# A Mamba block with experts on one core: the last row product of a block added to the sums by an accumulating DMA

## The chip, the cores and the metric

The kernel runs on one core of a Trainium2 chip, in one launch. The core's engines run side by side, each through its own list of instructions in order: TensorE (PE: matmuls and transposes; its weight loads are shown as PEld), VectorE (DVE), ScalarE (ACT), GpSimd (POOL) and SyncE (SP), which here only starts DMAs. They meet through semaphores alone: an instruction that waits holds up all that stands behind it on its engine. The metric is the time of one execution on the device in microseconds (us), lower is better.

## The reference

Only what bears on the change is kept. `x` has 16 sequences of 256 tokens by 256 features, E is 512, N is 16.

```python
xn = layernorm(x)
hidden, gate = split(einsum('blh,he->bel', xn, W_in), 2)
hidden = silu(causal_conv4(hidden) + conv_bias)              # 512 channels x 256 tokens
dt, B, C = split(hidden^T @ W_x, [128, 144])                 # 128, 16 and 16 columns
dts = softplus(dt @ W_dt + b_dt)
...
state[n] = exp(dts * A[n]) * state[n] + dts * B[n] * hidden  # a scan over tokens, for each n of 16
scan_out = sum over n of state[n] * C[n]
y = (scan_out + hidden * D) * silu(gate)
out = x + y^T @ W_out + experts(xn)                          # 32 experts, top 8, gate, up and down
```

All is float32. `experts` is computed densely: the 32 experts' 96 columns stand side by side as 24 tiles of 128, taken as 12 pairs.

## The kernel before

A block is one sequence. There are 16 of them, and their work is laid out in 128 slots a block (8 for each of the 16 states n). Every engine walks the same slots, and tables of numbers (`ROW_ADD_AT`, `WEIGH_AT` and others) say at which slot of which block each step stands in that engine's list. A table has three rows: for the first block, the fourteen in the middle, and the last. Slots under 0 belong to the block's early work and run while the block ahead is in its slots 0 to 127; slots of 128 and over run in the block behind. So slot -16 of the next block is slot 112 of this one, and slot 136 of this block is slot 8 of the next. The slots give an order and no time.

A state n goes like this. ScalarE makes the decays (`decays`, L657). GpSimd makes the input `du * B[n]` into one of four buffers (`state_input`, L571, `state[:, n % STATES]`, STATES is 4, 128 partitions x 1024 numbers). VectorE scans it in two halves (`scan`, L878). Then C[n] is applied in one of two ways. Eight states, 0 among them, go by turning: TensorE transposes them (`turn`, L1100) and VectorE multiplies and adds them into `acc` (`add_state`, L884). The other eight are the row states 2, 4, 5, 6, 8, 9, 10 and 12. For states 5 and 9 VectorE multiplies (L912) and adds (L919) from `decay`, which lies in PSUM. For states 2, 4, 6, 8, 10 and 12 GpSimd multiplies the state by a row of C laid over all partitions (`state_output`, L580), and VectorE adds the product, 128x1024, into the sums `u2` of the block (`add_row`, L891). Both inputs of that addition lie in SBUF. The sums are formed in a fixed order, `ROW_SUMS`, in which 12 is the last, behind 10. `y_sum` (L927) adds what was turned, GpSimd multiplies by the gate (`gated`, L591), and TensorE projects (`project_y`, L1148).

The buffer of state 12 is buffer 0. The next one to fill it is state 0 of the next block, at slot 112, and `state_input` waits there until the product of 12 has been added. `step_input` (L554, `du = u * dt` of the next block) stands just ahead of it on GpSimd, at slot 111. `weigh` (L586) multiplies a pair of expert tiles by their router weights, on GpSimd too. `norm` (L539 to L545) is GpSimd's part of the next block's normalization and waits for VectorE's `moments` (L826). `load_c` (L643) starts the loads of the rows of C from ScalarE's queue, and waits until GpSimd has made the product that used the buffer before.

Of the kernel before, what the change touches and what calls it, by code (L numbers as in the profile page):

```python
# [33 lines left out]
def build(nc, x_d, w_in_d, conv_k_d, conv_b_d, w_x_d, w_dt_d, b_dt_d, w_out_d, a_log_d, d_d,  # L34
# [33 lines left out]
    STATES = 4  # L68
# [45 lines left out]
    ROW_ADD_AT = [[42, 54, [45, 47], 70, 80, [76, 79], 106, 116], [37, 49, [44, 47], 61, 78, [76, 76], 102, 119], [30, 51, [43, 44], 64, 78, [75, 76], 102, 153]]  # L114
# [16 lines left out]
    ROWS_BY_VECTOR = [n for n in BY_ROW if n in ((5, 9))]  # L131
    ROW_SUMS = sorted(BY_ROW, key=lambda n: n if n in ROWS_BY_VECTOR else n + ROW_LAG)
# [19 lines left out]
    with ExitStack() as ctx:  # L152
# [6 lines left out]
        def sem(name):  # L159
            return ctx.enter_context(nc.semaphore(name))  # L160
# [133 lines left out]
        row_added = sem("row_added")  # L294
        row_summed = sem("row_summed")
# [75 lines left out]
        def row_at(i, n):  # L371

            of = [k for k in BY_ROW if k not in ROWS_BY_VECTOR]
            return i * len(of) + of.index(n) + 1

# [26 lines left out]
        def wait_summed(eng, i, k, h=1):  # L402

            if k < 0:
                eng.wait_ge(skip_ready, i + 1)
            elif ROW_SUMS[k] in ROWS_BY_VECTOR:
                eng.wait_ge(row_summed, row_half(i, ROW_SUMS[k], h))
            else:
                eng.wait_ge(row_added, row_at(i, ROW_SUMS[k]))

# [115 lines left out]
        def _(pool):  # L526
# [29 lines left out]
            def state_input(i, q, n):  # L556
# [6 lines left out]
                if not (isinstance(i, int) and i == 0 and n < STATES):  # L563
                    before, at = (n - STATES) % NS, (i if n >= STATES else i - 1)
                    if before in ROWS_BY_VECTOR:
                        pool.wait_ge(scanned, half_at(at, before, 1))
                    elif before in BY_ROW:
                        pool.wait_ge(row_added, row_at(at, before))
                    else:
                        pool.wait_ge(turned, turn_at(at, before, 1))  # L570
# [3 lines left out]
            def state_output(i, n):  # L574
# [5 lines left out]
                pool.tensor_tensor(x, x, c_rep[:, r % ROWS, :][:, None, :].broadcast_to([P, ET, T]), ALU.mult).then_inc(row_ready[0], 1)  # L580

# [11 lines left out]
            def slot(i, q, a):  # L593
# [8 lines left out]
                if a == POOL_ALONE[s]["rstd"]:  # L602
                    norm(i)
                if a == POOL_ALONE[s]["select"]:
                    select(i)
# [205 lines left out]
        def _(dve):  # L811
# [128 lines left out]
            def slot(i, q, a):  # L940
# [22 lines left out]
                for n, at in zip(BY_ROW, ROW_ADD_AT[s]):  # L963
                    if n not in ROWS_BY_VECTOR and a == at:
                        add_row(i, q, n)
# [250 lines left out]
```

## Time and profile before

| | us |
|---|---|
| median of 3 runs | 1341.82 |
| lowest and highest | 1341.73, 1341.94 |
| the profiled execution | 1342.44 |
| its span (first to last instruction) | 1340.6 |
| one block in the middle, by `gated` at 701.11 and 781.49 | 80.38 |
| TensorE busy in such a block (703.1 to 783.5) | 79.76 |
| VectorE, GpSimd, ScalarE busy in it | 76.66, 75.67, 75.15 |

The profiled execution took 1.8 us more than its span. The first block ramps up for some 60 us, the last ends at the end of the span, and the blocks between repeat each other. Busy times of TensorE come from modelled ends of pipelined matmuls. The clock granted to TensorE was full (0.999 as the mean of the span).

In a row of a timeline, "x2" means that two like instructions are merged; a bracket gives the engine's idle time just before and the instruction that ended it. ACTq and SPq are the queues of ScalarE and SyncE, whose DMA starts are rows of their own. A line's number is that of the kernel before.

### The profile page before, as it was taken

The page shows a single profiled execution, that of the slowest core. Times are in us where ns is not written, and L with a number is a line of the kernel's source. Part 1 is how long each engine was busy: PE and PEld are TensorE (multiplying, and loading weights), DVE is VectorE, ACT ScalarE, POOL GpSimd, SP SyncE. Part 2 cuts the span into 40 slices and gives each one's busy share as a digit, 9 for nine tenths or more (in the row PEclk, how much of TensorE's full clock was granted, in tenths as well). Part 3 has the DMA queues.
Part 4 walks back from the last instruction along what each step waited for, and adds up shares of the span by engine and source line. Part 5 has one row for each costly group of instructions (what it writes and reads, how often), then busy time and mean ns, then how long its engine had stood idle before and what let it go on. Part 6 is the DMA issues. An engine that isn't in the chain of part 4 may idle for free.

```text
span 1340.6 us, 26644 instructions
## 1 busy us (share of the span) xinstructions
PE 1301.6 (97%) x9222; PEld 1219.6 (91%) x9222; DVE 1239.6 (92%) x1644; ACT 1213.2 (90%) x2111; POOL 1233.9 (92%) x674
## 2 busy tenths in 40 slices
PE   6899999999999999999999999999999999999998
PEld 5889999999999999999999999999999899999987
DVE  3799999999999999999999999999999999999997
ACT  5879999999999999999999999999999899999984
POOL 2999999999999989999999999989999999999996
PEclk9999999999999999999999999999999999999999
DMA  7543443544444344443544444344443534434342
GB/s 193 160 144 118 143 120 115 152 115 132 139 127 135 112 136 127 139 120 118 149 120 126 136 128 138 114 132 131 139 122 116 148 114 134 139 113 142 109 146 80
DMA packets 189399, 174.95 MB, mean 130 GB/s; under 512 B 43185, under 2 KB 172241, under 8 KB 189265
## 3 DMA queue, kind: packets, MB, share of 16 engines
q1 hardware_dynamic: 150864, 121.86, 30.5%
q10 hardware_dynamic: 38400, 51.40, 13.6%
q8 instruction: 73, 1.20, 0.4%
q14 instruction: 62, 0.50, 0.1%
HBM read 167.92 MB, written 5.24 MB: 129 GB/s over the span
## 4 chain that ended last, share of the span: by engine, by line
POOL 27%; issue 21%; ACT 19%; DVE 18%; PE 12%; DMA 2%; ACTq 1%; SPq 0%; DVEq 0%; POOLq 0%
POOL state L571 14%; POOL moe L586 6%; ACT decay L657 5%; PE pair_ps L1003 5%; ACT L657 5%; ACT L665 4%; DVE state L878 4%; PE out_ps L1138 3%; POOL state L580 3%; DVE dt L865 3%; DVE u L891 2%; DVE decay L878 2%; DVE u L919 2%; ACT moe L665 2%; DVE moe L898 2%
## 5 line engine op out<-in xcount | busy, mean ns | idle before, releaser
L571 POOL TENSOR_TENSOR state<-du,b_rep 128x1024 f32<-128x1024 f32 x256 | 611.7, 2395 | 61.1 <-DVE u L891 59.3
L878 DVE TENSOR_TENSOR_SCAN state<-decay,state 128x512 f32<-128x512 f32 x448 | 534.2, 1212 | 21.1 <-ACT decay L657 16.4
L657 ACT ACTIVATE decay<-dt,neg_a 128x255 f32<-128x255 f32 x1024 | 436.7, 465 | 37.7 <-DVE state L878 19.0
L1138 PE MATMUL out_ps<-w_down,moe 128*128 128x256 f32 x1536 | 355.9, 381 | 3.1 <-POOL moe L586 1.9
L1138 PEld LDWEIGHTS out_ps<-w_down,moe 128*128 128x128 f32 x1536 | 282.5, 190 | 38.6 <-issue 4.1
L586 POOL TENSOR_TENSOR moe<-moe,rw_rep 128x512 f32<-128x512 f32 x192 | 249.3, 1309 | 8.7 <-DVE moe L898 7.3
L580 POOL TENSOR_TENSOR state<-state,c_rep 128x1024 f32<-128x1024 f32 x96 | 244.1, 2543 | 1.6 <-DVE state L878 1.6
L1003 PE MATMUL pair_ps<-xnT_hi,w_gate_hi 128*128 128x256 f32 x768 | 228.9, 298 | 3.2 <-DVE moe L898 3.2
L1003 PE MATMUL pair_ps<-xnT_hi,w_up_hi 128*128 128x256 f32 x768 | 225.7, 294 | 2.8 <-ACT moe L665 1.9
L657 ACT ACT_TABLE_LOAD x171 | 219.4, 1283 | 2.5
L1003 PE MATMUL pair_ps<-xnT_lo,w_gate_hi 128*128 128x256 f32 x768 | 216.4, 282 | 0.0
L1003 PE MATMUL pair_ps<-xnT_hi,w_gate_lo 128*128 128x256 f32 x768 | 216.0, 281 | 0.0
L1003 PE MATMUL pair_ps<-xnT_hi,w_up_lo 128*128 128x256 f32 x768 | 215.8, 281 | 0.0
L1003 PE MATMUL pair_ps<-xnT_lo,w_up_hi 128*128 128x256 f32 x768 | 215.7, 281 | 0.0
L665 ACT ACT_TABLE_LOAD x144 | 184.8, 1283 | 5.3 <-PE out_ps L1138 1.7
L884 DVE SCALAR_TENSOR_TENSOR acc<-turn_ps,c_tok,acc 128x512 f32<-128x512 f32 x224 | 160.4, 733 | 3.3 <-PE turn_ps L1100 2.1
L1003 PEld LDWEIGHTS pair_ps<-xnT_hi,w_up_hi 128*128 128x128 f32 x768 | 144.6, 188 | 12.2 <-ACT moe L665 8.1
L1003 PEld LDWEIGHTS pair_ps<-xnT_hi,w_gate_hi 128*128 128x128 f32 x768 | 145.3, 189 | 7.3 <-DVE moe L898 5.7
L891 DVE TENSOR_TENSOR u<-u,state 128x1024 f32<-128x1024 f32 x96 | 149.0, 1552 | 0.8 <-POOL state L580 0.2
L898 DVE TENSOR_TENSOR moe<-moe,pair_ps 128x512 f32<-128x512 f32 x192 | 129.2, 673 | 20.9 <-PE pair_ps L1003 20.9
L1003 PEld LDWEIGHTS pair_ps<-xnT_lo,w_gate_hi 128*128 128x128 f32 x768 | 145.4, 189 | 0.8
L1003 PEld LDWEIGHTS pair_ps<-xnT_hi,w_gate_lo 128*128 128x128 f32 x768 | 145.4, 189 | 0.0
(149 smaller groups left out, 2252.5 us busy)
## 6 DMA issues: line engine op xcount, KB each, us to landing
w_down<-in_L_ffn_w_down_dram SPq DMA_DIRECT2D x384, 128.0 KB, 2.9
b_rep<-b_dram ACTq DMA_DIRECT2D x128, 256.0 KB, 3.3
rw_rep<-rw_dram SPq DMA_DIRECT2D x256, 96.0 KB, 2.7
c_rep<-b_dram ACTq DMA_DIRECT2D x128, 128.0 KB, 3.3
rw_rep<-rw_dram SPq DMA_DIRECT2D x256, 64.0 KB, 2.6
rw_rep<-rw_dram SPq DMA_DIRECT2D x256, 32.0 KB, 2.6
x_in<-L_attn_input_states_dram SPq DMA_DIRECT2D x16, 256.0 KB, 3.8
res<-L_attn_input_states_dram SPq DMA_DIRECT2D x16, 256.0 KB, 3.1
```

The costliest lines, as they stand in the source:

```text
L571: pool.tensor_tensor(state[:, n % STATES, :, :], du2[:, q, :, :], b_rep[:, n // BCH % 2, n % BCH, :][:, None, :].broadcast_to([P, ET, T]), ...
L580: pool.tensor_tensor(x, x, c_rep[:, r % ROWS, :][:, None, :].broadcast_to([P, ET, T]), ALU.mult).then_inc(row_ready[0], 1)
L586: pool.tensor_tensor(moe[:, p % RING, :, :], moe[:, p % RING, :, :], rw_rep[:, p % WEIGHTS, :, :], ALU.mult).then_inc(pair_weighed[0], 1)
L657: last = act.activation(decay[:, h, j, 1:T], dt[:, q, e, 1:T], ACT.Exp, scale=neg_a[:, e, n:n + 1])
L665: act.activation(moe[:, p % RING, :, :], bank(p, 0), ACT.Silu).then_inc(pair_silu, 1)
L865: last = dve.scalar_tensor_tensor(out=x, in0=ps[:, j, 0:T - shift], scalar=conv_k[:, e, k:k + 1], in1=x, op0=ALU.mult, op1=ALU.add)
L878: dve.tensor_tensor_scan(a if n in ROWS_BY_VECTOR else x, a, x, 0.0, ALU.mult, ALU.add).then_inc(scanned, 1)
L884: dve.scalar_tensor_tensor(out=acc[:, c, :], in0=turn_ps[:, c, :], scalar=c_tok[:, q, c, NS + n:NS + n + 1], in1=acc[:, c, :], op0=ALU.mul ...
L891: dve.tensor_tensor(u2[:, q, :, :], u2[:, q, :, :], state[:, n % STATES, :, :], ALU.add).then_inc(row_added, 1)
L898: dve.tensor_tensor(m, m, bank(p, 1), ALU.mult).then_inc(pair_mul, 1)
L1003: last = pe.matmul(out, w(a, k), x(b, k), start=(at == 0), stop=(at == len(terms) - 1))
L1138: last = pe.matmul(out_ps[:, c, :], moe[:, p % RING, j, c * P:(c + 1) * P], w_down[:, p % RING, j, :], start=(p == 0 and j == 0 and c == 0 ...
```

## The change

The product of state 12 is no longer added by VectorE. GpSimd starts a DMA that reads `state[:, 0]` and adds it into `u2` in SBUF (`accum_op`), 128 partitions of 4 KB. It does so for each of the 16 blocks. A new semaphore, `row_moved`, tells when it has landed. What waited for the addition of 12 waits for it now: `state_input` of state 0 of the next block, and `y_sum`. The DMA start itself waits for the sum of row 10 (VectorE) and for GpSimd's own product of 12. It stands at slot 106, 102 or 118 (first, middle, last blocks), where VectorE's addition stood at 116, 119 or 153.

```diff
-    ROW_ADD_AT = [[42, 54, [45, 47], 70, 80, [76, 79], 106, 116], [37, 49, [44, 47], 61, 78, [76, 76], 102, 119], [30, 51, [43, 44], 64, 78, [75, 76], 102, 153]]
+    ROW_ADD_AT = [[42, 54, [45, 47], 70, 80, [76, 79], 106, 106], [37, 49, [44, 47], 61, 78, [76, 76], 102, 102], [30, 51, [43, 44], 64, 78, [75, 76], 102, 118]]
...
+    ROWS_BY_DMA = [n for n in BY_ROW if n in ((12,))]
...
+        def moved_at(i, n):
+
+            return (i * len(ROWS_BY_DMA) + ROWS_BY_DMA.index(n) + 1) * 16
...
+            elif ROW_SUMS[k] in ROWS_BY_DMA:
+                eng.wait_ge(row_moved, moved_at(i, ROW_SUMS[k]))
...
+                    elif before in ROWS_BY_DMA:
+                        pool.wait_ge(row_moved, moved_at(at, before))
...
+            def move_row(i, q, n):
+
+                wait_summed(pool, i, ROW_SUMS.index(n) - 1)
+                row_multiplied(pool, i, n)
+                pool.dma_start(u2[:, q, :, :], state[:, n % STATES, :, :], accum_op=ALU.add).then_inc(row_moved, 16)
...
+                for n, at in zip(BY_ROW, ROW_ADD_AT[s]):
+                    if n in ROWS_BY_DMA and a == at:
+                        move_row(i, q, n)
...
                 for n, at in zip(BY_ROW, ROW_ADD_AT[s]):
-                    if n not in ROWS_BY_VECTOR and a == at:
+                    if n not in ROWS_BY_VECTOR and n not in ROWS_BY_DMA and a == at:
                         add_row(i, q, n)
```

GpSimd's list in a middle block, from the product of 12 (the first row) to state 0 of the next block (the last), before. L571 makes state inputs, L586 weighs.

```order
L580 TENSOR_TENSOR state<-state,c_rep 128x1024 [waits c_loaded1,scanned]
L571 TENSOR_TENSOR state<-du,b_rep 128x1024 [waits row_added,b_loaded1]
L586 TENSOR_TENSOR moe<-moe,rw_rep 128x512 [waits pair_mul,rw_loaded0]
L586 TENSOR_TENSOR moe<-moe,rw_rep 128x512 [waits pair_mul,rw_loaded1]
L571 TENSOR_TENSOR state<-du,b_rep 128x1024 [waits turned]
L554 TENSOR_TENSOR du<-u,dt 128x1024 [waits dt_ready]
L571 TENSOR_TENSOR state<-du,b_rep 128x1024 [waits row_added,b_loaded0,du_ready]
```

The same place after:

```order
L590 TENSOR_TENSOR state<-state,c_rep 128x1024 [waits c_loaded1,scanned]
L581 TENSOR_TENSOR state<-du,b_rep 128x1024 [waits row_added,b_loaded1]
L602 TENSOR_TENSOR moe<-moe,rw_rep 128x512 [waits pair_mul,rw_loaded0]
L596 DMA u<-state 128x1024 [waits row_ready_by_pool,row_added]
L602 TENSOR_TENSOR moe<-moe,rw_rep 128x512 [waits pair_mul,rw_loaded1]
L581 TENSOR_TENSOR state<-du,b_rep 128x1024 [waits turned]
L562 TENSOR_TENSOR du<-u,dt 128x1024 [waits dt_ready]
L581 TENSOR_TENSOR state<-du,b_rep 128x1024 [waits row_moved,b_loaded0,du_ready]
```

The DMA start came in between two weighings, with one weighing, one state input and `du` between it and the instruction that waits for it. In the first block it stands one place on, behind the state input of 15, with only a weighing and `du` behind it. The second place is the end of VectorE's list in the last block, before (L891 is the addition of row 12, L927 is `y_sum`):

```order
L891 TENSOR_TENSOR u<-u,state 128x1024 [waits row_ready_by_pool,row_added]
L884 SCALAR_TENSOR_TENSOR acc<-turn_ps,c_tok,acc 128x512 [waits added,turned]
L898 TENSOR_TENSOR moe<-moe,pair_ps 128x512 [waits pair_silu,up_in]
L884 SCALAR_TENSOR_TENSOR acc<-turn_ps,c_tok,acc 128x512 [waits added,turned]
L898 TENSOR_TENSOR moe<-moe,pair_ps 128x512 [waits pair_silu,up_in]
L927 TENSOR_TENSOR u<-u,turn_ps 128x512 [waits row_added,y_turned] x2
```

and after:

```order
L917 TENSOR_TENSOR moe<-moe,pair_ps 128x512 [waits pair_silu,up_in]
L903 SCALAR_TENSOR_TENSOR acc<-turn_ps,c_tok,acc 128x512 [waits added,turned]
L917 TENSOR_TENSOR moe<-moe,pair_ps 128x512 [waits pair_silu,up_in]
L946 TENSOR_TENSOR u<-u,turn_ps 128x512 [waits row_moved,y_turned] x2
```

The addition is gone from the list, and `y_sum` waits for `row_moved` in place of `row_added`. The lists of TensorE, ScalarE and SyncE are the same in both kernels.

## Rows read from the trace of the kernel before

**Rows 1.** Busy times by stretch, one middle block; columns in the first line.

```profile
core 0: us, PE busy (x) PEld busy (x) DVE busy (x) ACT busy (x) POOL busy (x), PEclk, DMA share, GB/s
703.10:783.50 80.40, 79.76 (x569) 74.87 (x568) 76.66 (x104) 75.15 (x132) 75.67 (x42) 1.00 0.43 128
```

**Rows 2.** The chain that ended last, 700 to 800 us: start, us, what.

```profile
743.60 1.24 DVE u L891
...
744.96 0.51 POOL state L571
...
775.40 0.21 POOL var_eps L539
...
787.47 2.34 POOL state L580
789.88 0.33 ACTq L643
```

**Rows 3.** Timeline of GpSimd in one middle block: start, us, instruction.

```profile
754.43 3.38 POOL L580 TENSOR_TENSOR state<-state,c_rep 128x1024 f32<-128x1024 f32 x1
...
760.11 2.52 POOL L586 TENSOR_TENSOR moe<-moe,rw_rep 128x512 f32<-128x512 f32 x2
762.59 2.38 POOL L571 TENSOR_TENSOR state<-du,b_rep 128x1024 f32<-128x1024 f32 x1
764.93 3.34 POOL L554 TENSOR_TENSOR du<-u,dt 128x1024 f32<-128x1024 f32 x1
768.35 7.11 POOL L571 TENSOR_TENSOR state<-du,b_rep 128x1024 f32<-128x1024 f32 x3
```

**Rows 4.** Timeline of VectorE in the same block.

```profile
754.12 1.44 DVE L891 TENSOR_TENSOR u<-u,state 128x1024 f32<-128x1024 f32 x1
...
763.86 2.19 DVE L891 TENSOR_TENSOR u<-u,state 128x1024 f32<-128x1024 f32 x1
765.98 1.21 DVE L878 TENSOR_TENSOR_SCAN state<-decay,state 128x512 f32<-128x512 f32 x1
...
774.74 0.25 DVE L826 BATCH_NORM_AGGREGATE moments<-stats 128x2 f32<-128x6 f32 x2
...
776.01 1.26 DVE L927 TENSOR_TENSOR u<-u,turn_ps 128x512 f32<-128x512 f32 x2
```

**Rows 5.** Durations min/median/max in ns over the whole run, three lines.

```profile
L554 POOL TENSOR_TENSOR du<-u,dt x16: 2357/3342/3382, 37.3 to 1247.8; 128x1024 f32<-128x1024 f32 x16
L891 DVE TENSOR_TENSOR u<-u,state x96: 1197/1394/2276, 69.9 to 1325.9; 128x1024 f32<-128x1024 f32 x96
L445 SPq DMA_DIRECT2D x_in<-L_attn_input_states_dram x16: 428/432/979, 0.7 to 1111.8; - x16
```

**Rows 6.** DMA issues: count, KB each, median us from issue to landing.

```profile
u<-in_L_attn_W_in_dram SPq DMA_DIRECT2D x1, 512.0 KB, 4.3
gate<-in_L_ffn_w_up_dram SPq DMA_DIRECT2D x1, 384.0 KB, 6.9
neg_a<-in_L_attn_A_log_dram SPq DMA_DIRECT2D x1, 32.0 KB, 2.3
```

**Rows 7.** Busy times of a 4 us stretch, columns as in rows 1.

```profile
761.00:765.00 4.00, 4.00 (x36) 3.98 (x35) 4.00 (x5) 3.96 (x5) 4.00 (x4) 1.00 0.40 118
```

**Rows 8.** GpSimd's timeline at the end of the first block.

```profile
119.72 1.30 POOL L586 TENSOR_TENSOR moe<-moe,rw_rep 128x512 f32<-128x512 f32 x1
```

**Rows 9.** GpSimd's timeline at the end of the last block.

```profile
1322.87 2.40 POOL L580 TENSOR_TENSOR state<-state,c_rep 128x1024 f32<-128x1024 f32 x1
1328.54 2.54 POOL L586 TENSOR_TENSOR moe<-moe,rw_rep 128x512 f32<-128x512 f32 x2 [3.28 <-DVE moe L898]
1331.17 2.35 POOL L591 TENSOR_TENSOR u<-u,gate 128x1024 f32<-128x1024 f32 x1
```

**Rows 10.** VectorE's timeline there.

```profile
1329.81 1.28 DVE L927 TENSOR_TENSOR u<-u,turn_ps 128x512 f32<-128x512 f32 x2 [0.15 <-PE turn_ps L1110]
```

**Rows 11.** The chain that ended last, there: start, us, what.

```profile
1333.66 3.65 PE out_ps L1148 x16
```

More of the change, by code:

```diff
@@ L294, in build @@
         row_added = sem("row_added")
+        row_moved = sem("row_moved")
         row_summed = sem("row_summed")
@@ L371, in row_at @@
         def row_at(i, n):
-            of = [k for k in BY_ROW if k not in ROWS_BY_VECTOR]
+            of = [k for k in BY_ROW if k not in ROWS_BY_VECTOR and k not in ROWS_BY_DMA]
             return i * len(of) + of.index(n) + 1
+        def moved_at(i, n):
+            return (i * len(ROWS_BY_DMA) + ROWS_BY_DMA.index(n) + 1) * 16
         def read_a(i, name):
```

## The prediction

> **What bounds the kernel now.** Read the middle blocks first, since fourteen of the sixteen are alike. In one of them TensorE is busy for 79.76 of 80.40 us, and VectorE, ScalarE and GpSimd for some 75 to 77 [rows 1]. So nothing can win more than 0.6 us a block, TensorE's whole idle time, and there is no engine with much to spare for a loss either. The busy shares don't say which engine sets the pace, and the chain of waits does. In each block it comes from VectorE's addition of a row at 743.60 to GpSimd at 744.96, stays on GpSimd (apart from pieces named "issue", which lie inside instructions of GpSimd) until its product of row 2 ends at 789.8, and goes on to ScalarE's queue, whose start of a load of C waits for that product [rows 2]. In those 45 us GpSimd's timeline has no idle bracket; the stretch that the change touches, 754 to 775, is in the middle of it [rows 3]. A microsecond more of GpSimd there is a microsecond more for the block, and a microsecond less is worth at most 0.4: VectorE delivers the moments at 774.99, GpSimd picks them up at 775.40 [rows 2, 4], and from there on GpSimd would wait.
>
> **What the addition costs now.** VectorE's 128x1024 addition takes 1.2 us by itself (minimum 1197 ns) [rows 5]. At 763.86 it took 2.19, and GpSimd's `du`, begun at 764.93, took 3.34 in place of 2.36 [rows 3 to 5]. The times fit a turn-taking: the addition begins while GpSimd still runs the state input of 762.59 to 764.97, does its work only after that (764.97 to 766.05), and `du` starts in earnest only then. The same pair is at 754.12 and 754.43 (3.38 in place of 2.36). The median of `du` is 3342 ns over 16 blocks, so nearly every block pays this 1.0 us, on the path. The Trainium skill (SBUF — State Buffer, section "Who interferes with whom") states this: a VectorE instruction with two SBUF inputs and a GpSimd instruction that reads SBUF exclude each other. By that rule, the trace agrees, and the scans, whose decays lie in PSUM, cost GpSimd nothing.
>
> **What the change takes away.** On VectorE 2.19 us a block. It is not on the path: behind it stands the scan of state 15 (765.98), whose input GpSimd finishes at 764.97 now. On GpSimd 1.0 us a block, the waiting of `du`. It is on the path.
>
> **What it adds on GpSimd: the DMA's start (call it g).** The trace of before has no DMA begun by GpSimd. Nearest below: starts on the hardware queues of the other two, 0.33 us on ScalarE's [rows 2] and 0.43 on SyncE's [rows 5]. Nearest above: a whole GpSimd instruction over the same tile, 2.37 [rows 3]. Less than 0.33 is not likely, since GpSimd's work over a tile takes twice VectorE's time (2.36 to 1.20) [rows 5]. I scale SyncE's 0.43 by that 2, and by 1.5 because an accumulating transfer names three operand streams (two read, one written) against two: 1.3, and I take 1.2. Its two waits are met: row 10 was added by 755.56, and the product of 12 ended at 757.81, while the start would fall at 761.4, between the two weighings of 760.11. What is queued behind it is the second weighing, the input of 15, `du`, and state 0 of the next block. All of it moves by g - 1.0 = 0.2 us by the time state 0 starts. The input of 15 itself moves from 764.97 to 766.2, which holds VectorE's scan to 766.2 where it began at 765.98: VectorE gets nothing of its 2.19 us here.
>
> **What it adds as a wait: the landing (L, from the beginning of the start).** A load of 512 KB landed 4.3 us after issue and one of 32 KB took 2.3 [rows 6]. That leaves 2.0 for the data. The accumulating one reads both operands, so I double that: 2.3 + 4.0 = 6.3, plus 0.8 by which GpSimd's start is longer than SyncE's: L = 7.1. Bounds: 4.3 if reading twice costs nothing and the start is short; 2.3 + 2 x 4.6 = 11.5 if the worst large load of the trace (6.9, rows 6) is what it meets [rows 6]. Ahead of state 0 there is g, a weighing 1.25, an input 2.35 and `du` 2.36 (freed of its waiting), that is g + 6.0 = 7.2 us. So in a middle block the DMA lands 0.1 us before it is needed. That is no margin: past it, each us of L is a us of wait on GpSimd, on the path. The other waiter, `y_sum` at 776.01 [rows 4], has over 7 us of room. The removed addition had 2.3 us of room there (ended 766.05, needed 768.35).
>
> A page gives another price. The Trainium skill (DMA: Bandwidth & Descriptors, section "Anatomy of one DMA — SWDGE (gpsimd) path") puts a DMA begun by GpSimd at about 2.0 us plus its bytes at 436 GB/s, an estimate of 3.2 us here, and its specifications give about 1 us to the first byte. No run here shows it; it is weighed as a rival below, there worked out from rows.
>
> **The two ends.** First block: only a weighing 1.25 and `du` 2.36 stand between the start and state 0 [rows 5, 8], so the room is g + 3.6 = 4.8, the wait 2.3, and with the 0.2 of above 2.5 us. Last block: the product of 12 ends at 1325.27 and GpSimd has nothing to do until 1328.54, so g is free there, but the sum is needed by `y_sum`, which began at 1329.81, and `gated` and the projection follow at once (1331.17 + 2.35 = 1333.52, projection at 1333.66) [rows 9 to 11]. The DMA lands at 1325.27 + 7.1 = 1332.4, so `y_sum` is 2.6 late, of which 0.14 is room: 2.4 us. VectorE's addition did this in 1.22 us. Here is the one place where the latency of the DMA is in full on the path.
>
> **The sum.** Fourteen middle blocks x 0.2 = 2.8; first block 2.5; last block 2.4; together 7.7. On the profiled execution's 1342.44 that is 1350.1. The median of the runs is 0.6 below the profiled one, so 1349.5, that is 0.6% slower. The two blocks at the ends carry more than half of it.
>
> **The rivals.** (1) The start is as short as on the hardware queues. With g = 0.4 GpSimd gets 0.6 us a block, of which 0.4 counts before VectorE's moments hold it. The point from which the sign turns is g = 0.6 or so, as 14 x (g - 1.0) must pay for the ends. With L = 4.8 the first block pays 0.2 and the last 0.1. Sum 14 x -0.4 + 0.3 = -5.3, so 1336.5. For it: TensorE's 0.6 idle us allow it, and VectorE's freed 2.19 us could help where I see no use for them. Against: everything must go right, and GpSimd's programs are slow elsewhere in the trace. (2) Break-even: g = 1.0 and a landing within the room in all blocks. The ends then cost nothing when L is under 4.5 (1325.27 + 4.5 = 1329.8), the middle nothing: 1341.8. For it: the transfer begins where the DMA engines are 0.40 busy [rows 7], and 512 KB landed in 4.3 at the start of the run, where loads crowd. Against: an accumulate reads twice as much. The Trainium skill (the page and section above) leads to this case, with its estimate of 3.2 us. (3) The transfer is late: state 0 waits in every block. With L 1.5 us longer than mine, 8.6, the room of 7.2 is passed by 1.4, so 14 x 1.4 + 2 x 1.5 = 22.6 more: 1372. For it: it begins with no margin, a large load has taken 6.9 [rows 6], and the kernel's own loads take 0.44 of the DMA engines' time [rows 1] and share them. (4) The start itself is as long as a full instruction, g = 2.4: 14 x 1.4 = 19.6, and 5 at the ends: 1366, with the room grown to 8.4 so that no landing is waited for.
>
> **Chances.** My forecast and its neighbourhood (1345 to 1358) 0.38; (3) and (4) together 0.22, both slower; (2) 0.20, within 0.2%; (1) 0.20, faster. I take 0.2% (2.7 us) as what a measurement of this kernel can tell from no change. The range goes from 1336, the floor of (1), to 1371: over it lie the landings that are later still, up to 11.5, some 1 in 10, and under it less than 1 in 10. Faster 0.20, same 0.20, slower 0.60.
>
> **What the profile of the changed kernel would show.** The first thing to read is the row of GpSimd's DMA start, its duration g, and how far the next weighing begins after the last one ended. `du` at 2.36 in place of 3.34 in the middle blocks shows the freed microsecond; if it stays at 3.3, another addition has moved onto it. An idle bracket of GpSimd before state 0, released by the DMA, would show a late landing, and its absence would kill (3). The step between two `gated` instructions, 80.38 now, should be 80.6; under 80.1 is (1). In the last block the idle bracket before `y_sum` should name the DMA, with about 2.5 us. The forecast is wrong if GpSimd's stretch from 745 to 790 gets idle time of another cause, for then it did not set the pace.

## The result and the profile after

| | before | after |
|---|---|---|
| median of the runs, us | 1341.83 | 1355.15 |
| lowest and highest | 1341.73, 1341.94 | 1354.07, 1355.86 |
| the profiled execution, and its span | 1342.44, 1340.6 | 1354.85, 1353.0 |
| step from `gated` to `gated`, the block shown | 80.38 | 81.04 (709.07 to 790.11) |
| median of the 12 steps from the second to the thirteenth | 80.40 | 81.04 |
| first `gated` | 137.79 | 139.77 |
| last step | 68.13 | 69.11 |

The changed kernel is slower: ratio 1.0099, 95% interval 1.0081 to 1.0116. The direction and the range were right; the forecast of 1349.5 was 5.7 us short. Executions of one kernel differ by up to some 5 us with the mean clock granted to TensorE: on the chip of experiments 9 to 12 the kernel before has a median of 1342.57 us in its 19 executions at 0.999 or more and of 1347.72 in its 7 at 0.996 or less. Line numbers below are those of the changed kernel unless said otherwise: `state_input` is L581, `state_output` L590, the DMA start L596, `weigh` L602, `du` L562, the load of B L654, the decays L676, SiLU L684, the experts' matmul L1022.

The page of after, busy time and the issues of the new DMA (count, KB each, median us from issue to landing):

```profile
PE 1302.9 (96%) x9222; PEld 1219.0 (90%) x9222; DVE 1210.8 (89%) x1628; ACT 1213.2 (90%) x2111; POOL 1234.2 (91%) x690
...
u<-state POOLq DMA_DIRECT2D x16, 512.0 KB, 5.7
```

GpSimd's timeline in a middle block, the place of [rows 3]:

```profile
762.38 3.40 POOL L590 TENSOR_TENSOR state<-state,c_rep 128x1024 f32<-128x1024 f32 x1
765.72 2.38 POOL L581 TENSOR_TENSOR state<-du,b_rep 128x1024 f32<-128x1024 f32 x1
768.06 1.28 POOL L602 TENSOR_TENSOR moe<-moe,rw_rep 128x512 f32<-128x512 f32 x1
769.28 0.90 POOL L596 DMA_DIRECT2D u<-state  x1
769.94 1.58 POOL L602 TENSOR_TENSOR moe<-moe,rw_rep 128x512 f32<-128x512 f32 x1
771.19 2.64 POOL L581 TENSOR_TENSOR state<-du,b_rep 128x1024 f32<-128x1024 f32 x1
773.51 2.62 POOL L562 TENSOR_TENSOR du<-u,dt 128x1024 f32<-128x1024 f32 x1
776.21 7.08 POOL L581 TENSOR_TENSOR state<-du,b_rep 128x1024 f32<-128x1024 f32 x3
783.99 0.20 POOL L547 TENSOR_TENSOR var_eps<-moments,eps 128x2 f32<-128x2 f32 x1 [0.70 <-DVE moments L845]
```

From the product of 12 to state 0 GpSimd takes 13.83 us (762.38 to 776.21), where it took 13.92 (754.43 to 768.35) [rows 3]. So GpSimd itself lost nothing: the start took 0.66 between starts and left the three instructions behind it ending 0.27 later, together 0.93, and `du` no longer waits 1.0 for VectorE. State 0 has no bracket: the DMA had landed. Yet `var_eps` now has a wait of 0.70 for VectorE's moments. It had none at 775.40 [rows 2]. That wait, less the 0.09, is nearly all of the block's 0.66 us.

Who made the moments late stands in a place that no row of the prediction showed, ScalarE. Its timeline before, where L635 is the load of B and L657 the decays:

```profile
764.56 0.87 ACT L657 ACTIVATE decay<-dt,neg_a 128x255 f32<-128x255 f32 x2
765.06 0.33 ACTq L635 DMA_DIRECT2D b_rep<-b_dram  x1
765.43 0.48 ACT L657 ACTIVATE decay<-dt,neg_a 128x255 f32<-128x255 f32 x1
```

and after, with one instruction more:

```profile
772.27 0.87 ACT L676 ACTIVATE decay<-dt,neg_a 128x255 f32<-128x255 f32 x2
773.91 0.33 ACTq L654 DMA_DIRECT2D b_rep<-b_dram  x1
774.29 0.48 ACT L676 ACTIVATE decay<-dt,neg_a 128x255 f32<-128x255 f32 x1 [1.15 <-POOL state L581]
...
776.47 1.09 ACT L684 ACTIVATE moe<-pair_ps 128x512 f32<-128x512 f32 x2
```

The load of B overwrites the half of `b_rep` that the inputs of states 14 and 15 were made from, so its start waits until GpSimd has made the input of 15. Before, that input ended at 764.97 and the start followed at 765.06: no slack at all. After, it ended at 773.83 and the start followed at 773.91. A DMA start stands in ScalarE's list like any other instruction, and two exponentials, a table load of 1.28 us and the SiLUs stand behind it. TensorE waits for the SiLU, VectorE for TensorE, and the moments stand on VectorE's list behind that:

```profile
777.12 0.39 PE L1022 MATMUL pair_ps<-xnT_hi,w_up_hi 128*128 128x256 f32 x1 [1.01 <-ACT moe L684]
...
778.85 0.69 DVE L917 TENSOR_TENSOR moe<-moe,pair_ps 128x512 f32<-128x512 f32 x1 [1.28 <-PE pair_ps L1022]
...
783.60 0.25 DVE L845 BATCH_NORM_AGGREGATE moments<-stats 128x2 f32<-128x6 f32 x2
```

Measured from the start of the product of 12 (754.43 before, 762.38 after), the load of B starts 0.90 later than before, the exponential behind it (765.43 before) 0.91, and the moments (774.74 before) 0.91. In this block GpSimd had 0.27 of slack there (experiment 1), and 0.91 - 0.27 = 0.64 is the step's growth (0.66 here, 0.64 by the medians).

The chain that ended last goes the same way (start, us, what). It leaves GpSimd at the input of 15, which it did not do before [rows 2]:

```profile
769.28 0.90 POOL u L596
...
771.52 2.32 POOL state L581
...
773.91 0.33 ACTq L654
...
776.47 0.61 ACT moe L684
...
777.12 3.10 PE pair_ps L1022 x24
```

The waits of the whole run say that it is so in every block (engine and line, waited for: us in total, times, longest). Before:

```profile
DVE state L878 <- POOL state L571: 2.6, 3, 1.6
PE pair_ps L1003 <- ACT moe L665: 1.9, 5, 0.8
ACT decay L657 <- POOL state L571: 1.9, 1, 1.9
POOL var_eps L539 <- DVE moments L826: 7.1, 2, 6.9
```

After:

```profile
DVE state L897 <- POOL state L581: 31.6, 18, 2.1
ACT decay L676 <- POOL state L581: 15.9, 15, 1.9
POOL var_eps L547 <- DVE moments L845: 15.6, 14, 6.8
PE pair_ps L1022 <- ACT moe L684: 15.0, 19, 1.4
POOL state L581 <- DMA u<-state: 2.6, 1, 2.6
```

At the two ends the DMA is waited for. The first block on GpSimd:

```profile
119.32 1.06 POOL L596 DMA_DIRECT2D u<-state  x1
...
126.65 7.08 POOL L581 TENSOR_TENSOR state<-du,b_rep 128x1024 f32<-128x1024 f32 x3 [2.62 <-DMA u<-state]
```

and the last block on GpSimd and on VectorE:

```profile
1337.62 0.88 POOL L596 DMA_DIRECT2D u<-state  x1 [0.55 <-POOL state L590]
...
1342.15 1.28 DVE L946 TENSOR_TENSOR u<-u,turn_ps 128x512 f32<-128x512 f32 x2 [0.68 <-DMA u<-state]
```

The spans differ by 12.4 us. By `gated` they come from: the first block 1.98, the step after it 2.36, the twelve steps from there 7.16 (0.60 each), the last two steps -0.13 and 0.98, the end 0.05. The 2.36 belong to this execution more than to the change: the clock granted to TensorE was at 0.66 and 0.50 from 136 to 140 us (0.50 is 1.2 of 2.4 GHz), after a stretch of 2 us in which TensorE had been busy for 0.94. The same stop without that dip is in experiments 5 and 12; in the latter, the same kernel again, the step is 81.09, so 1.69 of the 2.36 go with the dip. The profiled execution of before has a dip of this kind too, elsewhere (0.57 in 60 to 64 us), and after has a second (0.57 in 24 to 28).

### The profile page after: what moved, and what is told of

The parts are those of the page before. It is cut to its first block, busy times and chain, and to the rows that moved or that the text cites. A ratio compares the mean times of both kernels' runs of the same rounds, so it can differ in the third digit from the quotient of the medians.

```text
span 1353.0 us, 26644 instructions
## 1 busy us (share of the span) xinstructions
PE 1302.9 (96%) x9222; PEld 1219.0 (90%) x9222; DVE 1210.8 (89%) x1628; ACT 1213.2 (90%) x2111; POOL 1234.2 (91%) x690
## 4 chain that ended last, share of the span: by engine, by line
ACT 28%; issue 18%; PE 17%; POOL 17%; DVE 16%; ACTq 2%; DMA 2%; POOLq 0%; SPq 0%; DVEq 0%
PE pair_ps L1022 9%; ACT decay L676 8%; POOL state L581 8%; ACT L676 6%; POOL moe L602 5%; ACT L684 4%; DVE state L897 4%; PE out_ps L1157 3%; ACT moe L684 3%; DVE u L910 3%; DVE dt L884 2%; DVE decay L897 2%; POOL state L590 2%; DVE u L938 2%; PE turn_ps L1119 2%
## 5 line engine op out<-in xcount | busy, mean ns | idle before, releaser
L581 POOL TENSOR_TENSOR state<-du,b_rep 128x1024 f32<-128x1024 f32 x256 | 615.1, 2409 | 68.0 <-DVE u L910 63.3
L676 ACT ACTIVATE decay<-dt,neg_a 128x255 f32<-128x255 f32 x1024 | 436.9, 465 | 46.6 <-DVE state L897 20.0
L602 POOL TENSOR_TENSOR moe<-moe,rw_rep 128x512 f32<-128x512 f32 x192 | 254.2, 1331 | 4.7 <-DVE moe L917 1.9
L590 POOL TENSOR_TENSOR state<-state,c_rep 128x1024 f32<-128x1024 f32 x96 | 244.0, 2542 | 1.5 <-DVE state L897 1.5
L1022 PE MATMUL pair_ps<-xnT_hi,w_up_hi 128*128 128x256 f32 x768 | 225.4, 294 | 15.1 <-ACT moe L684 15.0
L1022 PE MATMUL pair_ps<-xnT_hi,w_gate_hi 128*128 128x256 f32 x768 | 228.1, 297 | 3.8 <-DVE moe L917 3.8
L1022 PE MATMUL pair_ps<-xnT_lo,w_gate_hi 128*128 128x256 f32 x768 | 215.9, 281 | 0.0
L1022 PE MATMUL pair_ps<-xnT_hi,w_up_lo 128*128 128x256 f32 x768 | 215.8, 281 | 0.0
L1022 PE MATMUL pair_ps<-xnT_lo,w_up_hi 128*128 128x256 f32 x768 | 215.8, 281 | 0.0
L1022 PE MATMUL pair_ps<-xnT_hi,w_gate_lo 128*128 128x256 f32 x768 | 215.4, 280 | 0.0
L1022 PEld LDWEIGHTS pair_ps<-xnT_hi,w_up_hi 128*128 128x128 f32 x768 | 144.7, 188 | 26.6 <-ACT moe L684 21.8
L1022 PEld LDWEIGHTS pair_ps<-xnT_hi,w_gate_hi 128*128 128x128 f32 x768 | 144.8, 189 | 8.0 <-DVE moe L917 6.4
L1022 PEld LDWEIGHTS pair_ps<-xnT_lo,w_gate_hi 128*128 128x128 f32 x768 | 144.8, 189 | 0.8
L1022 PEld LDWEIGHTS pair_ps<-xnT_lo,w_up_hi 128*128 128x128 f32 x768 | 144.8, 189 | 0.2
L1022 PEld LDWEIGHTS pair_ps<-xnT_hi,w_gate_lo 128*128 128x128 f32 x768 | 144.8, 189 | 0.0
```

Of the source, the lines that this page charges most:

```text
L581: pool.tensor_tensor(state[:, n % STATES, :, :], du2[:, q, :, :], b_rep[:, n // BCH % 2, n % BCH, :][:, None, :].broadcast_to([P, ET, T]), ...
L602: pool.tensor_tensor(moe[:, p % RING, :, :], moe[:, p % RING, :, :], rw_rep[:, p % WEIGHTS, :, :], ALU.mult).then_inc(pair_weighed[0], 1)
L676: last = act.activation(decay[:, h, j, 1:T], dt[:, q, e, 1:T], ACT.Exp, scale=neg_a[:, e, n:n + 1])
L1022: last = pe.matmul(out, w(a, k), x(b, k), start=(at == 0), stop=(at == len(terms) - 1))
```

## The experiments

The theory: the time goes where GpSimd's start of the DMA delays the input of state 15, from there through ScalarE's queued load of B and back to GpSimd through the moments. The rivals: the DMA's own traffic or landing costs it; VectorE's lost 16 additions cost or give something unforeseen; the ends carry it. All kernels are edits of the changed one, but for experiments 4 and 11. "Step" is that of the block shown above, with the median of the twelve middle steps behind it.

**1. The product of 12 left out of the sums: no addition, no DMA.** The last of the six row products that GpSimd makes is missing in the output.

```diff
-                eng.wait_ge(row_moved, moved_at(i, ROW_SUMS[k]))
+                eng.wait_ge(row_added, row_at(i, 10))
...
-                        pool.wait_ge(row_moved, moved_at(at, before))
+                        wait_product(pool, at)
...
-                wait_summed(pool, i, ROW_SUMS.index(n) - 1)
-                row_multiplied(pool, i, n)
-                pool.dma_start(u2[:, q, :, :], state[:, n % STATES, :, :], accum_op=ALU.add).then_inc(row_moved, 16)
+                pass
```

> The changed kernel with the DMA taken out and nothing in its place: the product of row 12 is made, but not added to the sums, and the two that waited for the DMA wait for the product and for the sum of row 10. It shows what taking the addition from VectorE is worth. Theory of the held queue (GpSimd's start of 0.9 us puts off the input of state 15, ScalarE's queue waits for that input to start a load of B, and everything on ScalarE behind it is late): nothing is put off here, du takes 2.36 in place of 3.34, and the block gains what it can before VectorE's moments bind, 0.3 to 0.6 us: step between two gated instructions 79.8 to 80.1, ratio to before 0.993 to 0.997. Theory that the DMA's traffic is what costs: the same here. Theory that the addition's removal itself upsets the order of VectorE and GpSimd: 1.000 or above, step 80.4 to 81.

Measured 0.9979, interval 0.9965 to 0.9993; step 80.11 (80.23). GpSimd's timeline:

```profile
763.15 2.35 POOL L566 TENSOR_TENSOR du<-u,dt 128x1024 f32<-128x1024 f32 x1
...
773.34 0.20 POOL L551 TENSOR_TENSOR var_eps<-moments,eps 128x2 f32<-128x2 f32 x1 [0.66 <-DVE moments L847]
```

`du` is at 2.35, so VectorE's addition did cost it 1.0 us. Of that this block gets only 0.27, since the moments hold `var_eps` from there on (0.66). The gain is not the same in all blocks: six of the twelve middle steps take 80.07 to 80.13, the other six 80.33 to 80.55 (why is open), so it is 0.18 by the medians, and the 2.7 us of the whole run are 0.2 a block. That is what taking the addition from VectorE gives with these lists, the DMA free of charge.

**2. The same, with small GpSimd work of 0.75 us at the DMA's place.**

```diff
+                pool.wait_ge(started, 2)
+                pool.tensor_tensor(fill[:, 0:2], eps[:, :], minus_half[:, :], ALU.pow)
+                pool.memset(fill[:, 2:18], 0.0)
+                pool.memset(fill[:, 18:34], 0.0)
```

> As the one without the addition, but GpSimd runs three small instructions on a scratch tile (a power over 128x2 and two memsets of 128x16, together some 0.9 us) at the place where the DMA was started. Row 12 is not added, and there is no DMA by GpSimd. Held queue: the same loss as the changed kernel in the middle blocks, step 80.9 to 81.1, an idle bracket of about 1 us on ScalarE released by the input of state 15, and at the ends about nothing; ratio 1.006 to 1.009. Traffic theory: no transfer, so the step is below 80.4 and the ratio at most 1.000.

Measured 1.0046, interval 1.0029 to 1.0063; step 80.85 (80.86). The fill and the weighing behind it, on GpSimd:

```profile
765.47 0.71 POOL L600 TENSOR_TENSOR fill<-eps,minus_half 128x2 f32<-128x2 f32 x1
766.10 0.14 POOL L601 MEMSET fill<- 128x16 f32 x1
766.14 0.14 POOL L602 MEMSET fill<- 128x16 f32 x1
766.22 1.33 POOL L608 TENSOR_TENSOR moe<-moe,rw_rep 128x512 f32<-128x512 f32 x1
```

There is no transfer here at all, and 0.74 of the 0.75 us come back in the step of this block (0.63 by the medians), with the same waits: ScalarE's exponential for the state input in 15 blocks, TensorE for the SiLU 19 times. GpSimd's occupation is enough to make the loss; traffic isn't needed.

**3. The load of B six slots later.** Only ScalarE's list moves.

```diff
-                    if a == Q * BCH * (c - 2):
+                    if a == (-10 if c == 1 else Q * BCH * (c - 2)):
```

> The changed kernel, in which ScalarE starts the second load of B of a block at slot -10 in place of -16, behind the decays of state 15 and one silu. Held queue: ScalarE's idle bracket of 1.15 us goes, TensorE's idle 1.0 before the pair at 777.12 goes, step 80.2 to 80.5, ratio to before 1.000 to 1.004 (the two ends, some 3 us, stay). Theory that GpSimd's own lengthening sets the pace: no change from the changed kernel, step 81.0, ratio 1.0095. Traffic theory: no change either.

Measured 1.0016, interval 1.0001 to 1.0031; step 80.33 (80.34). ScalarE's timeline:

```profile
769.67 1.67 ACT L676 ACTIVATE decay<-dt,neg_a 128x255 f32<-128x255 f32 x4
771.13 0.33 ACTq L654 DMA_DIRECT2D b_rep<-b_dram  x1
```

All four exponentials run ahead of the start, TensorE's waits for the SiLU fall from 15.0 to 1.6 us, and `var_eps` waits no more. VectorE still waits 19.3 us in total for state inputs, and nothing comes of it. The 0.7 us of the block hung on one DMA start's place in ScalarE's list.

**4. The same move on the kernel before.**

> The kernel before with that one move alone (the second load of B at slot -10). Held queue: the input of state 15 was ready just as ScalarE came to that load, so nothing is waited for and nothing is won: 0.998 to 1.001, step 80.3 to 80.4. If the move by itself were worth more, to 0.995, its effect on the changed kernel would be no evidence.

Measured 1.0010, interval 0.9994 to 1.0026; median step 80.42. The move is worth nothing by itself, so in experiment 3 it undid a loss and brought no gain of its own.

**5. The weighing ahead of the input of 15 put behind it** (in the list of the middle blocks and of no other).

```diff
-                [17, 29, 37, 44, 65, 66, 80, 91, 99, 103, 131, 133],
+                [17, 29, 37, 44, 65, 66, 80, 91, 99, 105, 131, 133],
```

> The changed kernel with the weighing of pair 9 moved from slot 103 to 105, behind the input of state 15, in the middle blocks: the list is weighing, DMA start, input of 15, weighing, du, state 0. Held queue: the input of 15 is now 0.3 us earlier than in the kernel before (0.93 - 1.25), ScalarE doesn't wait for it, TensorE's idle 1.0 us goes: step 80.1 to 80.4, ratio 1.001 to 1.004, the rest being the two ends. VectorE's idle of 2.1 us before the scan of 15 shrinks to 0.9 or less. Theory that GpSimd's own lengthening sets the pace: the sum of GpSimd's work is the same, so 81.0 and 1.0095.

Measured 1.0007, interval 0.9990 to 1.0024; step 80.39 (80.35). GpSimd:

```profile
763.47 0.93 POOL L596 DMA_DIRECT2D u<-state  x1
764.12 2.70 POOL L581 TENSOR_TENSOR state<-du,b_rep 128x1024 f32<-128x1024 f32 x1
766.49 1.56 POOL L602 TENSOR_TENSOR moe<-moe,rw_rep 128x512 f32<-128x512 f32 x1
```

The start, the transfer and its landing are as in the changed kernel; only what stands behind the start is another instruction, one that nobody is waiting for. The middle's loss is gone. First `gated` is at 139.86 and the step behind it is 80.50, at full clock throughout, though TensorE had its stop there as well (busy for 1.06 of 134 to 136 us). At a granted clock of 0.999 or more the median is 1344.80 us in seven executions, against 1342.62 in eleven of the kernel before: what is left is about the ends.

**6. The DMA start behind the input of 15 in the middle blocks**, slot 105 in place of 102.

> The changed kernel with the DMA started at slot 105 in the middle blocks, behind the input of state 15 and ahead of du. Held queue: the input of 15 is no longer put off, so ScalarE's idle bracket of 1.15 us goes. But the room for the landing shrinks from 6.9 us to 0.9 + 2.4 = 3.3, and the DMA lands 5.0 to 5.7 us after its start: GpSimd waits 1.7 to 2.4 us for it before state 0, in each block, and VectorE's scan of state 0, the moments and the block follow: step 81.8 to 82.5, ratio to before 1.015 to 1.028. The prediction's own model of the room says the same. If the ratio stays at 1.010 or under, a landing that is waited for is not on the path.

Measured 1.0353, interval 1.0319 to 1.0386, worse than expected; step 83.46 (83.75). GpSimd:

```profile
790.80 0.89 POOL L596 DMA_DIRECT2D u<-state  x1
...
797.37 7.02 POOL L581 TENSOR_TENSOR state<-du,b_rep 128x1024 f32<-128x1024 f32 x3 [3.27 <-DMA u<-state]
```

The input of 15 is on time, but now the landing is not, 6.5 us after the start. The wait is in 15 blocks, 49.7 us together. GpSimd's own chain without a wait gives 80.33 (experiment 3), and 80.33 + 3.27 = 83.6. What the expectation had too low was the landing: its median is 6.5 here against 5.7. The mean granted clock was 0.984 to 0.990 in these four executions, so a part of the 3.5% may be the clock's; that was not separated. So one place is too late for the landing and the other too early for ScalarE.

**7. A plain DMA in place of the accumulating one** (the sums are overwritten by the product).

```diff
-                pool.dma_start(u2[:, q, :, :], state[:, n % STATES, :, :], accum_op=ALU.add).then_inc(row_moved, 16)
+                pool.dma_start(u2[:, q, :, :], state[:, n % STATES, :, :]).then_inc(row_moved, 16)
```

> The changed kernel with a plain DMA in place of the accumulating one: the sums are overwritten by the product of row 12 and not added to, same bytes, same place. It prices accumulation. By the prediction's doubling of the data part (2.3 fixed and 2.0 more a reading) it should land about 2 us earlier, 3.7 in place of 5.7 from its start; if both readings overlap, within 0.5 us of 5.7. GpSimd's start: 0.9 if the length is set by the descriptors of one side, 0.6 if by the number of operand streams. Held queue: the step stays at 80.9 to 81.1 as long as the start is as long; traffic theory: the step shortens with the bytes read, to 80.7 or less.

Measured 1.0050, interval 1.0032 to 1.0069; step 80.75 (80.79). GpSimd:

```profile
771.42 0.63 POOL L596 DMA_DIRECT2D u<-state  x1
772.08 1.30 POOL L602 TENSOR_TENSOR moe<-moe,rw_rep 128x512 f32<-128x512 f32 x1
...
775.65 2.35 POOL L562 TENSOR_TENSOR du<-u,dt 128x1024 f32<-128x1024 f32 x1
```

The start is 0.63 in place of 0.92 (medians) and leaves its neighbours alone: the weighing is at 1.30 and `du` at 2.35, where they are at 1.58 and 2.62 behind an accumulating start. It lands after 3.6 us (median) in place of 5.7. Over half of the middle's loss is still there (80.79 against 80.40 and 81.04, medians), for the smaller occupation. This kernel changes the start and the traffic at once, so it doesn't part them; experiment 2 does.

Six kernels now stand side by side. GpSimd's time from the product of 12 to state 0, and the step:

| | product to state 0 | more than in 1 | step | more than in 1 |
|---|---|---|---|---|
| 1, nothing | 12.95 | | 80.11 | |
| 7, plain DMA | 13.57 | 0.62 | 80.75 | 0.64 |
| 2, small work | 13.66 | 0.71 | 80.85 | 0.74 |
| after | 13.83 | 0.88 | 81.04 | 0.93 |
| before | 13.92 | 0.97 | 80.38 | 0.27 |
| 3, load of B later | 13.82 | 0.87 | 80.33 | 0.22 |

In the first four the extra time lies ahead of the input of 15, and each us of it is a us of the step. By the medians of the twelve steps the last column reads 0.56, 0.63, 0.81, 0.18 and 0.11: the same order, 0.1 less, because experiment 1 has its slower steps. In before it lies in `du`, behind that input, and all but 0.27 is absorbed. Experiment 3 has the time ahead of the input too, but ScalarE doesn't ask for it.

**8. VectorE adds the product of 12 in the first and the last block**, at its old slots 116 and 153, and the DMA does so in the fourteen between. VectorE's two additions signal a semaphore of their own, `row_ended`.

```diff
-                    if n in ROWS_BY_DMA and a == at:
+                    if n in ROWS_BY_DMA and a == at and s == 1:
...
-                    if n not in ROWS_BY_VECTOR and n not in ROWS_BY_DMA and a == at:
+                    if n not in ROWS_BY_VECTOR and (n not in ROWS_BY_DMA or s != 1) and a == at:
```

> The changed kernel, but in the first and the last block VectorE adds row 12 as before (slots 116 and 153), and the DMA does so in the fourteen middle blocks. It prices the two ends. By the two traces: the wait of 2.6 us for the DMA at 126.65, the half clock at 136 to 140 behind it and the slower next step cost 2.0 + 1.7 us, and the wait at the last y_sum about 1.0: 3.5 to 5 us less than the changed kernel, ratio to before 1.006 to 1.008, with the middle step at 81.0 as there. If the ends cost nothing: 1.0095.

Measured 1.0070, interval 1.0049 to 1.0090; median step 81.05, last step 68.61. The middle stays as it was. The gain of some 4 us, by the ratios 1.0070 here and 1.0099 and 1.0101 of the changed kernel, is not exact: the intervals overlap. At a granted clock of 0.999 or more it is smaller: the three executions here took 1351.54, 1352.05 and 1352.08 us, the three of the changed kernel (on other chips) 1354.07, 1354.11 and 1355.46, so some 2 us.

**9. Both repairs: the ends by VectorE, and the weighing behind the input of 15.**

> The changed kernel with two edits: in the first and the last block VectorE adds row 12's product again, and in all blocks the weighing that stood ahead of row 15's input on GpSimd stands behind it, so that this input ends about as early as before although the start of the DMA stays ahead of it. By the theory (the time is lost where GpSimd's start of the DMA delays row 15's input and with it ScalarE's queued load and its next exponential) the middle step is 80.3, as it was with the weighing moved alone, and the ends give back the 2 to 3 us that the wait in the first block (3.2 in that run) and the last block (about 1) took: ratio 0.998 to 1.0005 against before. By the rival (the DMA's traffic or the delay of weighing costs time whatever its place) the ratio stays at 1.0007 or above.

The weighing is moved as in experiment 5, in the fourteen middle blocks (the expectation says all).

Measured 0.9994, interval 0.9980 to 1.0009; step 80.32 (80.37). First `gated` is at 137.48 and the last step takes 68.21. Against experiment 5, which differs only at the ends (139.86, 69.04), the DMA in the first block costs 2.4 us and in the last 0.8. The whole times agree: at a granted clock of 0.999 or more the medians are 1341.89 us (eight executions) and 1344.80 (seven), 2.9 apart.

**10. The ends by VectorE, and the load of B later.**

> The changed kernel with two other edits: VectorE adds row 12's product in the first and the last block, and ScalarE's queue starts the load of one b_rep six slots later, so that ScalarE doesn't wait for row 15's input. Theory: middle step 80.33, as with the later load alone, less the ends: ratio 0.999 to 1.001. If the ends give nothing, 1.0016 as with the later load alone.

Measured 0.9996, interval 0.9981 to 1.0010; median step 80.35. Two different ways of keeping the start out of ScalarE's way give the same time.

**11. The weighing moved in the kernel before.**

> The kernel before with the same weighing behind row 15's input, and nothing else. If the weighing's place is what made the changed kernel fast in that run, and not the room it makes for the DMA's start, then this is faster than before, 0.996 to 0.998. By the theory before had no wait there to take away: step 80.2 to 80.5, ratio 0.999 to 1.001.

Measured 1.0005, interval 0.9989 to 1.0021; median step 80.42. Nothing to gain without the DMA: the move made room, and that is all.

**12. The changed kernel again, beside the last three.**

> The changed kernel once more, on the same chip as the three others, so that they can be compared with it directly: 1.0099 expected, and in the profile whether the first block's stop of TensorE (136 us) brings the half clock again.

Measured 1.0101, interval 1.0080 to 1.0122; median step 81.07. In its profile TensorE had the stop in the first block (busy for 1.06 of 136 to 138 us and 0.90 of 140 to 142) with a granted clock of 1.00 from 124 to 150 us, and the step behind it took 81.09, not 82.78. This profile has its dips earlier (0.61 in 60 to 64 us, 0.52 and 0.62 in 80 to 88), and its first `gated` is at 145.70 and not 139.77. The stop is in all six profiles in which the DMA adds in the first block or copies there (after, experiments 3, 5, 6, 7 and 12), and in none of the others that were made from the changed kernel (1, 2, 8, 9 and 10). So the stop comes with the DMA in the first block, and the dip behind it only sometimes. Whether the stop makes a dip likelier is open.

No version that adds the product of 12 beats the kernel before by more than the intervals can tell. The best one (experiment 9) is its equal: its median step is 0.03 us shorter, and at a granted clock of 0.999 or more its median is 1341.89 us (eight executions) against 1342.57 (nineteen), 0.05% less.

## Why the prediction was right, and where its size was off

That the change makes the kernel slower was forecast for a reason that did not bring it about. Without ScalarE's wait the changed kernel is experiments 3 and 5, and they measure 1.0016 and 1.0007, within the 0.2% that the prediction itself counted as no change. What the prediction counted, with the sizes that were measured, gives at most 14 x 0.09 us less in the middle and some 3 us more at the ends, an estimate of 2 us or 0.1%. So the direction was luck in good part; what pushed the time clear of break-even is a wait that the prediction didn't have. Its own last sign says so: it called the forecast wrong if GpSimd's stretch got idle time of another cause, and `var_eps` has 0.70 us of it. The range (1336 to 1371) was so wide that it tells little, and even so the prediction's own figure for rival (3), 1372, lay outside it.

- **What bounds the block: right as far as it went.** "A microsecond less is worth at most 0.4": 0.27 (experiment 1; 0.18 by the medians). But it named one chain, straight down GpSimd's list, and there are two. The second leaves GpSimd at the input of 15 and comes back through ScalarE, TensorE and VectorE at `var_eps`. In the block shown it was 0.27 us shorter than the first.
- **The microsecond that `du` gets back: right.** 3.34 became 2.35 (experiment 1), and 2.62 behind the start of the DMA. That fits the turn-taking.
- **The start, g = 1.2: a little long.** 0.93 in effect, of which 0.27 show only as later ends of the three instructions behind it. Less the freed 1.0, GpSimd's list is 0.09 us shorter now, where 0.2 longer was forecast. With this alone the kernel comes near rival (2), the break-even: experiment 5.
- **The middle term, 14 x 0.2: this is the step that failed.** The prediction said "All of it moves by g - 1.0 = 0.2 us by the time state 0 starts", and looked at who needs the end of the stretch. It did see that the input of 15 moves by the full g, and followed it to one reader, VectorE's scan, where it found 0.2 us and no harm. The other waiter of the same semaphore is ScalarE's load of B. The order of ScalarE's list is unchanged, as the text on the change says, but its waits are on GpSimd's work, and this one had 0.09 us between the input's end and the start. The term is then g less the slack, 0.93 - 0.27 = 0.66 in the block shown: 14 x 0.66 = 9.2 in place of 2.8. The step was forecast at 80.6 and came at 81.04.
- **The landing, L = 7.1: the upper part of what was measured.** 4.4 to 7.2, median 5.7. Of its terms the doubling of the 2.0 us for the data holds (experiment 7: accumulating costs 2.1 more than a plain copy, 5.7 against 3.6), and the rest, 2.3 + 2.0 + 0.8 = 5.1, was too long against the 3.6. With a path of 6.93 from the start to state 0 (769.28 to 776.21) it is in time in every middle block, as forecast (by 0.1 us there, by 1.94 in the block shown, where it landed after 4.99), and rival (3) fell. Experiment 6 shows how little can be taken from that room: with 3.3 us from the start to the end of `du` (790.80 to 794.09), 15 blocks wait. The Trainium skill (DMA: Bandwidth & Descriptors, section "Anatomy of one DMA — SWDGE (gpsimd) path") gives 2.0 us plus the bytes at 436 GB/s, an estimate of 3.2 us here. The plain transfer comes near it (3.1 to 6.6, median 3.6); for the accumulating one the trace doesn't agree (never under 4.4).
- **The first block, 2.5: right.** A wait of 2.62 where 2.3 was forecast, and 2.4 in effect (experiments 5 and 9).
- **The last block, 2.4: too much, 0.5 to 0.8 measured.** From the start of the product of 12 to `y_sum` it is 7.47 us in the changed kernel (1334.68 to 1342.15) and 6.94 in the one before (1322.87 to 1329.81), so 0.53; by experiments 5 and 9 it is 0.8. L was taken as one number. It isn't: the landing was 7.17 after the start in the first block, 4.44 in the last, and from 4.99 to 5.95 in the fourteen middle blocks. Here are the first block, two of the middle (landings 5.95 and 4.99) and the last (columns as in rows 1, the last two are the share of the DMA engines' time, the new transfer's own part included, and GB/s):

```profile
119.30:126.60 7.30, 7.27 (x56) 6.85 (x54) 5.21 (x7) 6.75 (x10) 4.73 (x4) 1.00 0.90 225
445.10:451.05 5.95, 5.95 (x44) 5.69 (x44) 4.15 (x6) 5.22 (x8) 5.95 (x5) 1.00 0.78 188
769.28:774.28 5.00, 5.00 (x39) 4.79 (x38) 2.91 (x5) 3.82 (x5) 5.00 (x5) 1.00 0.86 194
1337.60:1342.10 4.50, 4.50 (x33) 3.98 (x33) 2.81 (x5) 0.00 (x0) 2.60 (x3) 1.00 0.66 140
```

  GB/s times us gives 1.64 MB moved in the first block's stretch, 1.12 and 0.97 in the two of the middle and 0.63 in the last, 0.52 of it the new transfer's own. So at the ends the landing goes with what else is moved. The share doesn't order the middle blocks: the busier stretch is the one with the earlier landing. What sets the landing there is open.

- **The sum.** With the terms as measured, 9.2 + 2.4 + 0.8 = 12.4 (12.1 with the 0.5), and the spans differ by 12.4. That fits better than it should: in this execution the twelve middle steps gave 0.60 each and not 0.66, and of the 2.36 of the step before them 1.69 go with the clock dip. The 7.7 of the forecast had two misses of opposite sign, 6.4 too little in the middle and 1.6 to 1.9 too much in the last block.

## What to carry to other kernels

When an instruction is put into a busy engine's list, follow every instruction behind it to **all** waiters of its semaphore, the DMA starts on other engines' queues first of all: such a start took a third of a us here and, while it waited, held up all the compute behind it. A microsecond taken from a later instruction doesn't pay for one put ahead of an earlier one if somebody branches off between the two. Work moved from one engine to a DMA is not gone: its start is paid on the engine that begins it, and here that engine was the one with less to spare at that place.

## What the runs showed of the hardware that was not expected

- An accumulating DMA of 128 x 4 KB within SBUF occupies GpSimd for 0.88 to 1.06 us (median 0.92), a plain one of the same shape for 0.59 to 0.76 (median 0.63). Behind the accumulating one the next three GpSimd instructions show some 0.27 us longer (1.58 for 1.30, 2.64 for 2.37, 2.62 for 2.35), behind the plain one they don't.
- Accumulating costs 2.1 us of latency over the plain transfer (5.7 to 3.6, medians), and the landing of the same transfer varies by 2.7 us within one execution (4.44 to 7.17), latest where most else was moved beside it (1.64 MB in all) and earliest where least was (0.63 MB).
- In the last block, where the start directly follows the product it needs, it begins 0.55 us after that product's end.
